# Modulated-convolution chain: a re-ordered prologue, and the edge columns in 64-column tiles inside the first two turns

## What is computed

```
s      = style @ mod_w.T + mod_b                       # per sample and layer
weight = SCALE * w * s[:, None, :, None]
demod  = rsqrt(sum(weight * weight, axis=(2, 3)) + EPS)
weight = weight * demod[:, :, None, None]
out    = conv(x, weight) + b                           # layer 1: transposed, then blur (1,3,3,1)/4
                                                       # layer 3: blur (1,3,3,1)/8, then stride 2
return x + out
```

## Time and profile before

| | |
|---|---|
| median of 3 runs | 169.01 us (168.2 to 170.15) |
| profiled execution | 168.33 us, span 166.5 us |
| mean granted TensorE clock | 0.987 of 2.4 GHz |
| PE busy | 158.8 us, 95% |
| DVE busy | 131.8 us, 79% |
| POOL busy | 94.4 us, 57% |
| ACT busy | 56.4 us, 34% |
| mean rate of the DMAs | 107 GB/s |

### The profile page before, as it was taken

The page is one execution under the profiler, slowest core; times in us unless marked ns, Lnnn a source line. Parts: engine busy times, 40 slices in busy tenths (PEclk is TensorE's granted clock), DMA queues, the critical chain, the costliest instruction groups (busy, mean ns, idle before and its releaser), DMA issues. The chain is left out here.

```text
span 166.5 us, 8946 instructions
## 1 busy us (share of the span) xinstructions
PE 158.8 (95%) x3975; PEld 146.1 (88%) x3975; DVE 131.8 (79%) x229; ACT 56.4 (34%) x127; POOL 94.4 (57%) x155
## 2 busy tenths in 40 slices
PE   7999999999999999999999999999999999999970
PEld 5687888959789789999899999999999999999960
DVE  7859877788868869778696969696979797969993
ACT  3245561323142332334251514243434334231120
POOL 7209908596493977456373829191919192837530
PEclk9959999999999999999999999999999999999998
DMA  4982000120302204335343445353634242030314
GB/s 119 274 212 14 2 4 4 55 79 4 125 8 65 68 4 126 130 130 190 105 183 118 182 133 186 129 193 111 213 110 145 88 143 101 7 126 4 132 74 180
DMA packets 13990, 17.81 MB, mean 107 GB/s; under 512 B 5216, under 2 KB 5760, under 8 KB 13952
## 3 DMA queue, kind: packets, MB, share of 16 engines
q1 hardware_dynamic: 13888, 17.22, 31.1%
q10 hardware_dynamic: 64, 0.02, 0.1%
HBM read 8.85 MB, written 8.39 MB: 104 GB/s over the span
## 5 line engine op out<-in xcount | busy, mean ns | idle before, releaser
L190 POOL TENSOR_TENSOR Hw<-Hw 128x192 f32<-128x192 f32 x15 | 9.0, 598 | 50.8 <-DVE Hw L885 50.8
L546 PE MATMUL p_m<-uu,Hw 64*64 64x128 f32 x992 | 31.6, 269 | 0.0
L546 PEld LDWEIGHTS p_m<-uu,Hw 64*64 64x64 f32 x992 | 29.4, 132 | 0.1
L466 PE MATMUL p_lo<-xin,w0s 64*64 64x259 f32 x384 | 27.7, 406 | 0.1
L309 POOL COPY Hw<-Hw 64x896 f32<-64x896 f32 x15 | 25.8, 1722 | 1.0
L466 PE MATMUL p_le<-xin,w0s 64*64 64x260 f32 x384 | 26.3, 389 | 0.0
L511 PE MATMUL p_le<-R_sb,F_st 64*64 64x128 f32 (+2 forms) x768 | 25.8, 266 | 0.3 <-issue 0.3
L536 PE MATMUL p_m<-u,Hw 64*64 64x256 f32 x384 | 25.4, 375 | 0.0
L896 DVE TENSOR_TENSOR uu<-u 128x516 f32<-128x516 f32 x32 | 24.3, 796 | 1.4
L911 DVE TENSOR_TENSOR e_sb<-p_lo,s_sb 128x512 f32<-128x512 f32 x16 | 11.1, 696 | 16.8 <-PE p_lo L546 16.6
L511 PEld LDWEIGHTS p_le<-R_sb,F_st 64*64 64x64 f32 x768 | 23.3, 133 | 1.1 <-issue 0.9
(11 more groups left out here) (140 smaller groups left out, 217.8 us busy)
## 6 DMA issues: line engine op xcount, KB each, us to landing
xin<-in_x_dram SPq DMA_DIRECT2D x32, 256.0 KB, 3.3
out_dram<-ot SPq DMA_DIRECT2D x32, 256.0 KB, 2.4
wn<-in_L_cond_weights_dram SPq DMA_DIRECT2D x1, 192.0 KB, 3.5
mwn<-in_L_cond_mod_w_dram SPq DMA_DIRECT2D x1, 128.0 KB, 2.2
xe<-in_x_dram SPq DMA_DIRECT2D x2, 56.0 KB, 7.7
cn<-in_cond_dram ACTq DMA_DIRECT2D x1, 16.0 KB, 2.0
bn<-in_L_cond_mod_b_dram ACTq DMA_DIRECT2D x1, 1.0 KB
bn<-in_L_cond_biases_dram ACTq DMA_DIRECT2D x1, 1.0 KB
```

Of the source, the lines that this page charges most:

```text
L466: ins = pe.matmul(bank[h * C:(h + 1) * C, s, 0:n], w0s[p % 2][rows, k, :], xin[p % NX][rows, i0:i0 + 2 * n - 1:2], start=(k == 0), stop=(k ...
L546: ins = pe.matmul(bank(h)[s * C:(s + 1) * C], tap(p, h, s, blk), moving(slice(h * C, (h + 1) * C), s, k), start=(k == 0), stop=(k == len(b ...
```

## The change

- The four warm-up matmuls and their tile go.
- Layer 0 of pair 0 starts before the transposes of wsum and the demodulation products, which stand between its three taps now; wsumT goes to p_le in place of p_lo. The F blocks stand before compose_R(0); the o blocks before compose_H(0) in place of after compose_R(1); w2T and yc after compose_H(0). ACT's copies follow that order.
- On DVE s0 comes before the sum of squares and the squared style; make_diffs(0) before demodulation(0, 2); demodulation(3, 4) after the blocks of pair 0, and make_uu(0) after edge_x0.
- edge_y, edge_z and the zc product are cut into matmuls of 64 output columns, and blocks that are zero are left out.
- edge_y stands before product_1_mid of turn 0, edge_z between the halves of layer 0 in turn 1, edge_out before product_1_mid of turn 1. The waits for s_made move with them. DVE's and POOL's steps follow: POOL does finish_x0 and finish_y before it sums and places pair 2, finish_z and finish_out before pair 3.
- `LATE` is 2, and only pair 1 is stored in between.

```diff
-    LATE = 4
+    LATE = 2
...
             for p in range(-1, PAIRS):
                 if p == 0:
                     finish_x0()
-                if p == 1:
                     finish_y()
-                if p == 2:
+                if p == LATE - 1:
                     finish_z()
-                if p == LATE - 1:
                     finish_out()
...
-            between = (1, 4, 7)
+            between = (1,)
...
-            pe.wait_ge(warm_made, 1)
-            for _ in range(4):
-                pe.matmul(p_le[:, 1, 0:256], pe_warm[:, 0:P], pe_warm[:], start=True, stop=True)
...
                 for k, rows in ((0, P), (2, C)):
-                    c = 4 - 2 * k
-                    ins = pe.matmul(p_e[:, 0:2 * B * 5], y_st[0:rows, c:c + 2, :].rearrange("p a c -> p (a c)"),
-                                    x0e[0:rows, :, :, k:k + 5], start=(k == 0), stop=(k == 2))
+                    for h in range(2):
+                        ins = pe.matmul(p_e[h * C:(h + 1) * C, 0:2 * B * 5], y_st[0:rows, 4 - 2 * k + h, :],
+                                        x0e[0:rows, :, :, k:k + 5], start=(k == 0), stop=(k == 2),
+                                        skip_group_check=True)
                 ins.then_inc(put["ye"], 1)
+
+            def z_blocks(h, first):
+
+                return (1, slice(0, P)) if first else (0, slice(C, P)) if h == 0 else (2, slice(0, C))
 
             def edge_z():
                 pe.wait_ge(made["ye"], 2)
-                for k in range(3):
-                    ins = pe.matmul(p_e[:, 0:2 * B * 4], z_st[:, k, :], ye[:, :, :, k:k + 4],
-                                    start=(k == 0), stop=(k == 2))
+                pe.wait_ge(made["e_read"], 4)
+                for first in (True, False):
+                    for h in range(2):
+                        k, rows = z_blocks(h, first)
+                        ins = pe.matmul(p_e[h * C:(h + 1) * C, 0:2 * B * 4], z_st[rows, k, h * C:(h + 1) * C],
+                                        ye[rows, :, :, k:k + 4], start=first, stop=not first, skip_group_check=True)
                 ins.then_inc(put["ze"], 1)
...
-            layer0_odd(0)
+
+            pe.wait_ge(w0s_made, 1)
+            pe.wait_ge(x_loaded[0], 32)
+            layer0(0, p_lo, NO, 1, lo_done, [0])
+            pe.wait_ge(made["wsum"], 1)
+            for l in range(LAYERS):
+                ins = pe.transpose(p_le[0:C, 0, l * C:(l + 1) * C], wsum[:, l, :], ident[0:C, 0:C])
+            ins.then_inc(put["wsumT"], 1)
+            layer0(0, p_lo, NO, 1, lo_done, [1])
+            pe.wait_ge(copied["wsumT"], 1)
+            pe.wait_ge(made["style2"], 1)
+            for l in range(LAYERS):
+                ins = pe.matmul(p_m2[0:C, 0, 256 + l * B:256 + (l + 1) * B], wsumT[:, l], style2[:, l, :],
+                                start=True, stop=True)
+            ins.then_inc(put["demod"], 1)
+            layer0(0, p_lo, NO, 1, lo_done, [2])
             layer0(0, p_le, NE, 0, le_done)
-            pe.wait_ge(copied["V_st"], 2)
-            compose_R(0)
 
 
             pe.wait_ge(made["cid"], 1)
             pe.wait_ge(made["dt"], 2)
             blurred_taps(1, p_m2[:, 1], cid2, NF).then_inc(put["FT"], 1)
+            pe.wait_ge(copied["V_st"], 2)
+            compose_R(0)
+            pe.wait_ge(copied["G_mv"], 1)
+            blurred_taps(3, b_m13[1], cid1, 3).then_inc(put["oT"], 1)
+            pe.wait_ge(copied["F_st"], 1)
+            compose_H(0)
             taps_transposed(2, b_m13[0], 256).then_inc(put["w2T"], 1)
+            compose_R(1)
             pe.wait_ge(made["vec"], 1)
...
-            pe.wait_ge(copied["F_st"], 1)
-            compose_H(0)
-            compose_R(1)
-            blurred_taps(3, b_m13[1], cid1, 3).then_inc(put["oT"], 1)
-
             layer0_odd(1)
             compose_H(1)
...
                     layer0_odd(p + 1)
+                    if p == 1:
+                        edge_z()
                     layer0_even(p + 1)
                 if p + 2 < PAIRS:
                     compose_R(p + 2)
 
-                if p < 4:
-                    pe.wait_ge(made["e_read"], 2 * (p + 1))
+                if p < 3:
+                    pe.wait_ge(made["e_read"], (2, 6, 8)[p])
                 product_2(p)
...
                 if p + 2 < PAIRS:
                     compose_H(p + 2)
-                product_1_mid(p)
-                product_3(p)
-                if p < 3:
+                if p < 2:
                     pe.wait_ge(s_made, p + 1)
                 if p == 0:
                     edge_y()
                 if p == 1:
-                    edge_z()
-                if p == 2:
                     edge_out()
+                product_1_mid(p)
+                product_3(p)
...
             then()
-            tt(style2[:], style[0:C], style[0:C], ALU.mult, "style2")
             ts(pvec[0:C, W_S0], style[0:C, 0, 0:B:2], 1.0)
             ts(pvec[C:P, W_S0], style[C:P, 0, 1:B:2], 1.0, name="s0")
+            step(dve.tensor_reduce(wsum[:], wsq[:], AX_X, ALU.add), "wsum")
+            tt(style2[:], style[0:C], style[0:C], ALU.mult, "style2")
...
+            make_diffs(0)
             demodulation(0, 2)
-            make_diffs(0)
...
-            make_uu(0)
-            demodulation(3, 4)
...
             tt(vec[:, V_A0, 0:B], dm[:, 1, :], dm[:, 0, :], ALU.mult)
+            demodulation(3, 4)
...
             edge_x0()
+            make_uu(0)
             dve.wait_ge(put["oc"], 1)
...
             for p in range(PAIRS):
+                if p == 1:
+                    edge_z()
                 if p + 1 < PAIRS:
                     make_diffs(p + 1)
                 if p + 1 < PAIRS:
                     make_uu(p + 1)
                 add_parts(p)
+                if p == 0:
+                    edge_y()
+                if p == 1:
+                    edge_out()
                 add_mid(p)
...
```

More of the change, by code:

```diff
@@ L384, in _ @@
                     load(p + 4, 1)
-                if LATE <= p < LATE + 6:
+                if LATE <= p < LATE + 2 * len(between):
                     sp.wait_ge(lo_done, p + 3)
@@ L440, in _ @@
             taps_transposed(0, b_m13[0], 0).then_inc(put["w0T"], 1)
[L442 to L445, removed]
             for a in range(K):
@@ L450, in _, with layer0 @@
             ins.then_inc(put["GT"], 1)
[L452 to L461, removed]
+            def layer0(p, bank, n, first, done, ks=range(K)):
+                for k in ks:
                     for s in range(2):
@@ L657, in _ @@
             pe.wait_ge(copied["w2T"], 1)
-            for k in range(3):
-                ins = pe.matmul(p_m13[:, 0, 0, 0:B], z_st[:, k, :], yc[:], start=(k == 0), stop=(k == 2))
+            for first in (True, False):
+                for h in range(2):
+                    k, rows = z_blocks(h, first)
+                    ins = pe.matmul(p_m13[h * C:(h + 1) * C, 0, 0, 0:B], z_st[rows, k, h * C:(h + 1) * C], yc[rows],
+                                    start=first, stop=not first, skip_group_check=True)
             ins.then_inc(put["zc"], 1)
@@ L718, in _ @@
             copy_both(w0T, p_m13[0:C, 0, 0, 0:3 * C].rearrange("p (k c) -> p k c", c=C), copied["w0T"])
-            act.wait_ge(put["wsumT"], 1)
-            copy(wsumT[:], p_lo[0:C, 0, 0:LAYERS * C].rearrange("p (l c) -> p l c", c=C), copied["wsumT"])
             def scale_w0(p):
@@ L760, in _ @@
             copy_both(G_mv, p_m13[0:C, 1, 0, 0:K * C].rearrange("p (a c) -> p a c", c=C), copied["G_mv"])
+            act.wait_ge(put["wsumT"], 1)
+            copy(wsumT[:], p_le[0:C, 0, 0:LAYERS * C].rearrange("p (l c) -> p l c", c=C), copied["wsumT"])
             act.wait_ge(made["dt"], 2)
             act.activation(dq[:], dt_[:], ACT.Sqrt).then_inc(sqrt_done, 1)
+            evac_odd(0)
             act.wait_ge(made["e2"], 1)
@@ L766, in _ @@
             make_A(0)
-            evac_odd(0)
-            act.wait_ge(made["e1"], 1)
-            evac_R(0)
             act.wait_ge(put["FT"], 1)
@@ L772, in _ @@
                            scale=1.0 / 32).then_inc(copied["F_st"], 1)
+            act.wait_ge(made["e1"], 1)
+            evac_R(0)
             make_A(1)
-            act.wait_ge(put["w2T"], 1)
-            copy(w2T[:], p_m13[0:C, 0, 1, 0:3 * C].rearrange("p (k c) -> p k c", c=C), copied["w2T"])
+            act.wait_ge(put["oT"], 1)
+            act.activation(o_st[:], p_m13[:, 1, 0, 0:3 * C].rearrange("p (a c) -> p a c", c=C), ACT.Copy,
+                           scale=0.125).then_inc(copied["o_st"], 1)
             scale_w0(1)
@@ L778, in _ @@
             evac_H(0)
+            act.wait_ge(put["w2T"], 1)
+            copy(w2T[:], p_m13[0:C, 0, 1, 0:3 * C].rearrange("p (k c) -> p k c", c=C), copied["w2T"])
             evac_R(1)
             make_A(2)
-            act.wait_ge(put["oT"], 1)
-            act.activation(o_st[:], p_m13[:, 1, 0, 0:3 * C].rearrange("p (a c) -> p a c", c=C), ACT.Copy,
-                           scale=0.125).then_inc(copied["o_st"], 1)
```

(8 more changed lines are left out.)

6 lines of the change are left out of this document (2 added, 4 removed).

## The result

The changed kernel took 171.28 us (median; the same number for the kernel before on the same chip is 169.01), a ratio of 1.0149, 95% interval [1.0104, 1.0194].

The account below looks back on a forecast made before the run. TensorE was taken as the bound from 9.5 us on. Turn 1 starting 1.1 us late, less 0.55 from edge_z, gave +0.55 on the median of 169.01: 169.6 us, range 167.2 to 171.3.

Parts of the forecast that it names:

- its likeliest case: Measured time between 167.3 and 170.7 us, not to be told from no change (about 1%, 1.7 us); chance 0.61.
- The edges on TensorE: edge_z, edge_y and the zc product in 64-column tiles save 0.55, 0.35 and 0.45 us: 1.35 us, between 1.0 and 1.6.
- The start: Prologue: s0 ready at 7.0, layer 0 starts at about 7.5, 1.8 us earlier; demodulation products end at 10.4, 0.9 later.
- R(1) loses its cover: Before layer0_odd(1): only yc (about 0.4 us) covers ACT's 0.73 us emptying of R(1); it starts at 21.1, 0.6 late.
- The new wait in turn 0: Before edge_y: TensorE waits for s_made(1) and x0e; edge_y starts at 32.6, turn 1 at 35.65, 1.1 us late.
- 12.4 us: VectorE's stretch from sum_taps(0) at 20.1 to the end of s_sb at 32.5, with demodulation(3, 4) and make_uu(0) moved in.
- the same contention that the prediction had used for the F copies: VectorE and GpSimd share one port pair exclusively; moving make_uu(0) away shortens POOL's 6.04 us chain to F_dup by 0.5.
- After that: Turn 1 onward: edge_z gives its 0.55 us; edge_out, a near thing, taken as no wait, up to 1 us if not.
- The stores cost nothing: On SP, stores starting two turns earlier, with waits before loads three turns ahead of use, are hidden and cost nothing.
- The clock did rise later: Rival, chance 0.15: without warm-up the low clock lasts another 3 us; 0.3 to 1.5 us more, 169.9 to 171.1.
- its signs of being wrong: In the changed profile: no gap before edge_y, the clock at half beyond 12 us, or a gap before edge_out.
- The waits don't bind: Rival, chance 0.20: DVE and POOL keep up, TensorE runs gapless from 7.5; 2.3 us faster, 166.7, or half, 167.8.

## Why the prediction was wrong

It had the direction (0.6 above before) and its range (167.2 to 171.3) held the time by 0.02 us, which is luck; its likeliest case was no measurable change, and the loss was four times as large. Two of its steps failed: when the demodulation chain starts, and how long VectorE needs up to s_sb. By its own steps:

**The edges on TensorE: right.** 1.35 us was forecast, bounds 1.0 to 1.6; 1.17 measured between the same two points. zc gave the 0.45 forecast, edge_y and edge_z 0.72 for 0.90: three slots of edge_y lie between 33.42 and 34.44, 0.34 each in place of 0.28. The Trainium skill (TensorEngine Tiling (Array Packing), Key Properties) says that a change of tiling mode drains TensorE. The slot across the change from 128x64 to 64x64 tiles took 0.37 us, its two neighbours 0.32, so by these rows a drain costs no more than 0.05 us.

**The start: failed, by 1 us.** "What layer 0 waits for is the scale s0" was the wrong wait. s0 was there at 7.43, 0.4 later than forecast, but the transposes of w0 (six matmuls, 6.33 to 7.23) had no place in the forecast: ACT's copies of them take until 7.93 and the scaling until 8.42. TensorE had also stood 1.09 us for the biases' transfer. Layer 0 started at 8.47, not 7.5 (7.9 to 8.2 in five variants with the same order). Its first third took 1.07, start to start, not 0.88. The products ended at 12.0, not 10.4: 1.0 of this from the start, 0.6 from the pieces between. POOL's chain started at 14.55, not 13.1. The chain itself was shorter than forecast, 5.04 for 5.5, and F was duplicated at 19.59 for 18.65. The stall in compose_H(0) was about 0.4 (no start between 19.22 and 19.65) for 1.1, as TensorE was late too. The tap sum started at 20.99 for 20.1: 0.9 of the error.

**R(1) loses its cover: right in size (0.50 for a gap of 0.5), worth nothing.** The run that gave the cover back was no faster: a longer wait behind it took up what it gave.

**The new wait in turn 0: right in kind and length, but late: VectorE's stretch failed, by 1.2 us.** The wait stands where it was forecast, 1.24 long for about 1.3, for s_sb and x0e. The term "12.4 us" for VectorE was exact for the two steps moved (12.42 in the run that moved only these), but the list of what was moved was incomplete: "w2T" went into the sum with its 0.65 us on TensorE alone. What hangs on it, POOL's z_st and xse, moved with it onto VectorE's block sums: 1.2 us more. This is the same contention that the prediction had used for the F copies, and it overlooked it one step later. From s_sb to edge_y's start it was 0.44, x0e's copy, where the forecast had 0.1. So edge_y came 2.45 late (35.05 for 32.6): 0.9, 1.2 and 0.35. The wait for zc (1.10), behind demodulation(3, 4) in the same queue, is the same lateness of VectorE seen earlier, and no further loss beside it.

**After that: right.** Turns 1 and 2 gave 0.44 for 0.55, edge_out did not wait (46.21, without a bracket). "The stores cost nothing" is neither refuted nor shown: 0.2 and 0.5% in two pairs, inside the intervals, and the profiles lean to 0.6 us.

**Rivals.** The clock did rise later, near 13.9 by the durations (see below), which the prediction had among its signs of being wrong. It decided nothing here: in the six profiles of this order without the warm-up and with the late demodulation the even half of layer 0 took 1.71 to 2.60 us, and F was duplicated at 19.06 to 19.59 in all of them. Turn 1 starts at 37.72 and 37.80 in two with 2.60, at 37.93 in the one with 2.06. "The waits don't bind" would have needed VectorE to have the 19% that the earlier trace rows seemed to show; the two moves made its stretch 1.5 us longer (12.42 for 10.93) and the collision another 1.2.

**What the loss consists of.** The prologue's order cost 2.3 to 2.8% against a gain of 1 to 1.5% by the tiles, with no warm-up. At the start of turn 3 the profiles account for it. The kernel with the old prologue and the new places is there at 52.65 to 53.21 (three profiles), with VectorE's new order at 54.48, the changed kernel at 57.18 (56.99 and 57.02 in the runs with the old stores and with the cover). That is 3.8 to 4.5 us. The runs that move one thing alone give 1.3 to 1.8 for VectorE's order (both directions), 1.3 to 1.5 for the late w2T and 0.8 to 1.0 for the late demodulation, together 3.4 to 4.3. In the medians VectorE's order is 0.9 to 1.2%, measured both ways; the late demodulation 0.6 to 0.7%, within the noise; and putting w2T back early gave nothing. Why a kernel that is 1.5 us ahead at turn 3 does not keep it stays open.

## What to carry to other kernels

When a step is moved, follow its result through to every consumer and put each on its new neighbours: a transpose priced at its 0.65 us on TensorE moved a GpSimd product onto VectorE's critical steps, and the stretch grew by 1.2. When work moves into a stretch bound by one engine, add up each other engine's queue from its first to its last step there; the 19% that VectorE seemed to have free did not hold the two steps moved in here. And price a start by all inputs of its first instruction, not by the one that the change improves.

## What was not expected of the hardware

- The granted clock on record did not show the low level. In the changed kernel it reads 1.00 from the start, but the even half of layer 0 took 12.55 to 14.61, 2.06 us, where the high level takes 1.39 and the low one 2.44 to 2.79. Its matmuls last 0.64 us up to 13.4 and 0.39 from 14.0 on, so the rise came near 13.9. Of the 17 profiles only that of the kernel before has a low stretch on record, yet the even half took from 1.38 to 2.60 us. It took 2.60 with the warm-up in the changed kernel and 1.39 without it in one of the old prologue: between these two it was not the warm-up that decided when the rise came.
- Two VectorE steps of 128x64 took 0.65 us in place of 0.22 beside GpSimd's product with two inputs, each ending 0.09 us after one of its instructions. The Trainium skill (SBUF — State Buffer, SBUF: two separate sides) describes an exclusive lock that a VectorE operation with two SBUF inputs and a GpSimd operation that reads SBUF take for the whole instruction. The 0.65 agrees with it. Beside GpSimd's short copies a step of 128x192 kept its 0.34, and the copy gave way, with 0.33 for 0.23.
